# The layer norms' averaging products from f32 to two f16 halves, in a fused FFN and delta-rule attention kernel

## The reference, cut to what matters

```
x = x + 0.5 * ffn(layernorm(x))                 # call "1"
x = x + attn_block(layernorm(x))                # a delta-rule scan over time, 16 heads of 16
x = x + 0.5 * ffn(layernorm(x))                 # call "2"

def layernorm(x):
    m = mean(x, -1);  v = var(x, -1)
    return (x - m) / sqrt(v + 1e-05)

def ffn(x):   # ternary weights, scales s
    h = silu(x @ w1 * s1) * (x @ w2 * s2)
    h = gelu(h @ h1 * s); h = gelu(h @ h2 * s)
    return h @ w3 * s3
```

## Time and profile before

| | |
|---|---|
| median of 3 runs | 1821.66 us (1820.79 to 1822.48) |
| the profiled execution | 1821.63 us, its span 1819.9 us |
| mean granted clock of TensorE | 0.993 of full speed |
| TensorE busy | 1735.8 us, 95% of the span |
| VectorE, GpSimd, ScalarE busy | 68%, 66%, 58% |
| data moved | 23.16 MB, mean 13 GB/s |

### The profile page before, as it was taken

How to read it: one execution, slowest core, us unless ns; L and a number is a source line. 1 busy time by engine, 2 the same in 40 slices (tenths; PEclk the granted TensorE clock), 3 DMA queues, 4 the chain that set the end, 5 groups by cost and what they waited for, 6 DMA issues and landing times.

```text
span 1819.9 us, 29744 instructions
## 1 busy us (share of the span) xinstructions
PE 1735.8 (95%) x10030; PEld 1070.0 (59%) x10030; DVE 1242.6 (68%) x2890; ACT 1059.9 (58%) x2115; POOL 1209.4 (66%) x1501
## 2 busy tenths in 40 slices
PE   6989989999999999999999999999999999999999
PEld 5865555555555555655555555588655555555578
DVE  5255777777776877867777787767776768767331
ACT  4656565465656565646557474757555565655454
POOL 4463876767676666777676667667775867775653
PEclk9999999999999999999999999999999999999999
DMA  7100000000000000000000000000000000000000
GB/s 281 51 1 1 1 1 1 1 1 2 0 2 1 24 1 24 1 1 1 1 1 1 1 24 1 12 13 1 1 1 1 1 1 13 1 1 12 1 13 13
DMA packets 5270, 23.16 MB, mean 13 GB/s; under 512 B 640, under 2 KB 1664, under 8 KB 3584
## 3 DMA queue, kind: packets, MB, share of 16 engines
q1 hardware_dynamic: 5120, 21.26, 3.2%
HBM read 17.06 MB, written 4.19 MB: 12 GB/s over the span
## 4 chain that ended last, share of the span: by engine, by line
PE 64%; issue 10%; POOL 10%; DVE 9%; ACT 7%; DMA 0%; POOLq 0%; DVEq 0%; ACTq 0%; SPq 0%
PE ffn_bank L1072 38%; PE ffn_bank L1055 7%; PE att_bank L1120 5%; PE att_bank L1092 4%; POOL hid_lo L564 4%; POOL pairs_lo L601 2%; PE state_bank L1128 2%; POOL pairs L593 2%; PE ln_bank L1023 2%; PE att_bank L1107 2%; PE att_bank L1108 2%; ACT hid L679 1%; DVE roots L798 1%; DVE hid L820 1%; PE att_bank L1137 1%
## 5 line engine op out<-in xcount | busy, mean ns | idle before, releaser
L1072 PE MATMUL ffn_bank<-hid_hi,w_sb 128*128 128x512 f16 (+1 forms) x2736 | 907.0, 347 | 8.3 <-ACT gate L666 4.7
L1072 PE MATMUL ffn_bank<-hid_lo,w_sb 128*128 128x512 f16 (+1 forms) x2736 | 906.8, 347 | 0.0
L564 POOL TENSOR_TENSOR hid_lo<-hid,hid_hi 128x512 f16<-128x512 f32 (+1 forms) x456 | 462.4, 1029 | 278.3 <-ACT hid_hi L655 277.8
L593 POOL TENSOR_TENSOR pairs<-KQ 128x32 f32<-128x32 f32 (+15 forms) x496 | 326.9, 667 | 146.4 <-DVE KQ L847 104.6
L1072 PEld LDWEIGHTS ffn_bank<-hid_hi,w_sb 128*128 128x128 f16 x2736 | 276.3, 101 | 208.1 <-issue 12.2
L1072 PEld LDWEIGHTS ffn_bank<-hid_lo,w_sb 128*128 128x128 f16 x2736 | 268.9, 98 | 206.3 <-issue 13.6
L601 POOL TENSOR_TENSOR pairs_lo<-pairs,pairs_hi 128x448 f16<-128x448 f32 (+15 forms) x416 | 313.1, 757 | 80.7 <-ACT pairs_hi L727 79.9
L727 ACT CAST pairs_hi<-pairs 128x448 f16<-128x448 f32 (+15 forms) x416 | 176.9, 438 | 200.4 <-POOL pairs L593 147.0
L655 ACT CAST hid_hi<-hid 128x512 f16<-128x512 f32 (+1 forms) x456 | 235.0, 552 | 28.5 <-DVE hid L820 27.8
L679 ACT ACTIVATE hid<-ffn_bank,par_sb 128x512 f32<-128x512 f32 (+1 forms) x304 | 172.2, 616 | 107.6 <-PE ffn_bank L1072 105.2
L1055 PE MATMUL ffn_bank<-xn_hi,w_sb 128*128 128x512 f16 (+1 forms) x608 | 204.8, 351 | 15.1 <-DVE w_sb L769 6.3
(11 more groups left out here) (88 smaller groups left out, 2101.7 us busy)
## 6 DMA issues: line engine op xcount, KB each, us to landing
NK<-in_w SPq DMA_DIRECT2D x11, 1024.0 KB, 6.3
X<-in_x SPq DMA_DIRECT2D x7, 512.0 KB, 3.5
out<-X SPq DMA_DIRECT2D x7, 512.0 KB, 2.6
wqkvb_sb<-in_wqkvb SPq DMA_DIRECT2D x1, 1024.0 KB, 9.1
X<-in_x SPq DMA_DIRECT2D x2, 256.0 KB, 6.7
out<-X SPq DMA_DIRECT2D x2, 256.0 KB, 2.1
wout_sb<-in_wout SPq DMA_DIRECT2D x1, 256.0 KB, 9.9
par_sb<-in_par SPq DMA_DIRECT2D x1, 24.0 KB, 2.5
```

The lines of the kernel that those rows point to most:

```text
L564: pool.tensor_tensor(hid_lo[layer % 2][:, m, call.cols], hid[:, u % 3, call.cols], hid_hi[layer % 2][:, m, call.cols], ALU.subtract).then_ ...
L593: pool.tensor_tensor(packed(pair(pairs, q, dot), n), later, earlier, ALU.mult).then_inc(pairs_made if dot in SPLIT else pairs_ready, 1)
L1072: mm = nc.tensor.matmul(ffn_ps(call, j), weight(name, kk, 2 * pair + i), v[:, kk, cols], start=kk == 0 and part == 0, stop=kk == KT_FF - 1 ...
```

## The change

- The norms in frames (33 of 35) no longer give the f32 sum to TensorE. ScalarE copies feature_sum to an f16 tile `sum_hi`, GpSimd subtracts to get the f16 rest `sum_lo`, and TensorE makes two f16 products with an f16 `average16`, which add up in the bank. So does the variance.
- The additions `sum` and `sq_sum` of the 17 FFN norms in frames go from GpSimd to VectorE. Those of the attention's and the head's norms stay.
- Ticks: the attention norm's `var` stands one tick later; half_ln is laid out anew (16 ticks to `low` where it was 15); the FFN norms of frames 1 and 4 stand at tick 55, not 52; the dot of step 6 of qk at 16, not 17; the copies to Kz two ticks earlier.
- `terms` is one buffer, not two. The qk dots take the matrix of minus ones, as the kk dots do, and O subtracts them. `average` lies in U_sb, which is free at that time. One small reduction at the start is gone (`side_ones`), and the f16 copy made there is that of `average`.

```diff
-E_QK = [1, 4, 6, 7, 12, 14, 17, 19, ...]
+E_QK = [1, 4, 6, 7, 12, 14, 16, 19, ...]
 def ffn_ln(at):
-    return dict(sum=at, mean=at + 4, center=at + 5, square=at + 6, sq_sum=at + 7, var=at + 11, root=at + 11,
+    return dict(sum=at, sum_hi=at + 1, sum_lo=at + 2, mean=at + 4, center=at + 5, square=at + 6, sq_sum=at + 7, sq_hi=at + 8, sq_lo=at + 9, var=at + 11, root=at + 11,
...
-LN_ATT = dict(sum=18, mean=22, center=24, square=25, sq_sum=27, var=30, root=32, recip=35, norm=37, y_recip=38, apply=38, low=39)
+LN_ATT = dict(sum=18, sum_hi=19, sum_lo=20, mean=22, center=24, square=25, sq_sum=27, sq_hi=28, sq_lo=29, var=31, root=32, recip=35, norm=37, y_recip=38, apply=38, low=39)
-LN_FFN = [(-1, 55), (0, 55), (1, 52), (2, 55), (4, 52), (5, 55), ...]
+LN_FFN = [(-1, 55), (0, 55), (1, 55), (2, 55), (4, 55), (5, 55), ...]
...
+        def on_pool(job):
+            return job.kind == "att" or job.frame is None
...
@@ gpsimd
-                if part == "sum":
+                if part == "sum" and on_pool(job):
...
-                if part == "sq_sum":
+                if part == "sq_sum" and on_pool(job):
...
+                if part in ("sum_lo", "sq_lo") and job.frame is not None:
+                    pool.wait_ge(ln_sum_hi, split_count(i, part))
+                    pool.tensor_tensor(sum_lo[:, cols], feature_sum[:, cols], sum_hi[:, cols], ALU.subtract).then_inc(ln_sum_lo, 1)
@@ scalar
+                if part in ("sum_hi", "sq_hi") and job.frame is not None:
+                    if part == "sum_hi":
+                        act.wait_ge(ln_summed, i + 1)
+                    else:
+                        act.wait_ge(ln_sq_summed, i + 1)
+                    act.copy(sum_hi[:, cols], feature_sum[:, cols]).then_inc(ln_sum_hi, 1)
...
-                        if e == E_RETR[c] + 8:
+                        if e == E_RETR[c] + 6:
                             make_kz(f, c)
@@ vector
+                if part == "sq_sum" and not on_pool(job):
+                    dve.wait_ge(ln_squared, i + 1)
+                    nc.vector.tensor_tensor(total, xn[:, 0:1, cols], xn[:, 1:2, cols], ALU.add).then_inc(ln_sq_summed, 1)
...
-                part = terms[:, m % 2, 0:2 * GB * n].rearrange("p (v g w) -> p v g w", v=2, g=GB)
+                part = terms[:, 0:2 * GB * n].rearrange("p (v g w) -> p v g w", v=2, g=GB)
...
-                nc.vector.tensor_tensor(O[:, mine], O[:, mine], O_in[:, :], ALU.add).then_inc(o_ready, 1)
+                nc.vector.tensor_tensor(O[:, mine], O[:, mine], O_in[:, :], ALU.subtract).then_inc(o_ready, 1)
@@ tensor
-                if part in ("mean", "var"):
-                    nc.tensor.matmul(ln_bank[:, 0:cols.stop - cols.start], average[:, :], feature_sum[:, cols], start=True, stop=True).then_inc(ln_filled, 1)
...
+                elif part in ("mean", "var"):
+                    pe.wait_ge(ln_sum_lo, split_count(i, part))
+                    nc.tensor.matmul(ln_bank[:, 0:n], average16[:, :], sum_hi[:, cols], start=True, stop=False)
+                    nc.tensor.matmul(ln_bank[:, 0:n], average16[:, :], sum_lo[:, cols], start=False, stop=True).then_inc(ln_filled, 1)
```

More of the change, by code:

```diff
@@ L306, in build @@
         U_sb = sb("U_sb", [P, COLS])
+        average = U_sb[:, 0:P]
         O = sb("O", [P, COLS])
@@ L319, in build @@
         Uz = sb("Uz", [P, GP, 2, 32])
-        terms = sb("terms", [P, 2, 2 * GB * C])
+        terms = sb("terms", [P, 2 * GB * C])
         state_bd = sb("state_bd", [P, GB, P])
@@ L365, in slab, with split_count @@
             return X[:, s % RING, :, cols]
+        def on_pool(job):
+            return job.kind == "att" or job.frame is None
+        def split_count(i, part):
+            return (i - len(JOB_HEAD)) * 2 + (1 if part in ("sum_hi", "sum_lo", "mean") else 2)
         def both(ap):
@@ L784, in ln @@
                 n = cols.stop - cols.start
+                total, xs = feature_sum[:, cols].unsqueeze(1), slab(job.s, cols)
+                if part == "sum" and not on_pool(job):
+                    if job.kind == "ffn1":
+                        dve.wait_ge(x_loaded, 16 * job.s)
+                    else:
+                        dve.wait_ge(att_read_v, READ["out", job.s * HALVES + (cols.stop - 1) // HALF, 0])
+                    dve.wait_ge(ln_normed, i)
+                    nc.vector.tensor_tensor(total, xs[:, 0:1, :], xs[:, 1:2, :], ALU.add).then_inc(ln_summed, 1)
+                if part == "sq_sum" and not on_pool(job):
+                    dve.wait_ge(ln_squared, i + 1)
+                    nc.vector.tensor_tensor(total, xn[:, 0:1, cols], xn[:, 1:2, cols], ALU.add).then_inc(ln_sq_summed, 1)
                 if part == "center":
@@ L1013, in ln @@
                 i, cols = job.i, job.cols
[L1015 to L1023 removed]
+                n = cols.stop - cols.start
+                if part == "mean" and i:
+                    pe.wait_ge(ln_read, i * 2)
+                if part in ("mean", "var") and job.frame is None:
+                    if part == "mean":
+                        pe.wait_ge(ln_summed, i + 1)
+                    else:
+                        pe.wait_ge(ln_sq_summed, i + 1)
+                    nc.tensor.matmul(ln_bank[:, 0:n], average[:, :], feature_sum[:, cols], start=True, stop=True).then_inc(ln_filled, 1)
+                elif part in ("mean", "var"):
+                    pe.wait_ge(ln_sum_lo, split_count(i, part))
+                    nc.tensor.matmul(ln_bank[:, 0:n], average16[:, :], sum_hi[:, cols], start=True, stop=False)
+                    nc.tensor.matmul(ln_bank[:, 0:n], average16[:, :], sum_lo[:, cols], start=False, stop=True).then_inc(ln_filled, 1)
             def bank_free(call, j):
@@ L1105, in dots @@
                 if dot in SPLIT:
-                    i, ones = SPLIT[dot], head_ones16 if dot[0] == "qk" else head_minus16
-                    nc.tensor.matmul(ps[:, 0:n], ones[:, :], pair(pairs_hi, i, dot), start=True, stop=False)
-                    nc.tensor.matmul(ps[:, 0:n], ones[:, :], pair(pairs_lo, i, dot), start=False, stop=True).then_inc(att_filled, 1)
+                    i = SPLIT[dot]
+                    nc.tensor.matmul(ps[:, 0:n], head_minus16[:, :], pair(pairs_hi, i, dot), start=True, stop=False)
+                    nc.tensor.matmul(ps[:, 0:n], head_minus16[:, :], pair(pairs_lo, i, dot), start=False, stop=True).then_inc(att_filled, 1)
                     return
-                nc.tensor.matmul(ps[:, 0:n], (head_ones if dot[0] == "qk" else head_minus)[:, :], pair(pairs, DOT[dot], dot), start=True, stop=True).then_inc(att_filled, 1)
+                nc.tensor.matmul(ps[:, 0:n], head_minus[:, :], pair(pairs, DOT[dot], dot), start=True, stop=True).then_inc(att_filled, 1)
             def retrieve(w, c):
```

34 lines of the change are left out of this document (13 added, 21 removed).

## The result

| | before | changed |
|---|---|---|
| median | 1821.89 us (1820.79 to 1822.48) | 1847.7 us (1843.85 to 1849.85) |
| ratio | | 1.0138 [1.0126, 1.0151] |
| profiled execution, its span | 1821.63, 1819.9 us | 1847.51, 1845.8 us |
| mean granted clock | 0.993 | 0.990 |

The change costs 26 us. I had said 7 us faster and a range up to 1829: wrong in sign and outside the range. (Times are medians of undisturbed executions; one of e1_f32's five took 5100.91 us and is left out, so its median is 1814.04 us, where the expectations on record have 1815.85.)

A forecast was written before the change was run, and what follows sets the result against it. TensorE, 95% busy and 64% of the chain, was taken as the bound. -19.8 + 5.6 + 2.1 + 2.6 + 2.5 + 1.7 - 1.6 = -6.9 us gave 1814.7 us, range 1801 to 1829.

The forecast's parts named there:

- Loads: Added copies, subtractions and additions on ScalarE, GpSimd and VectorE: costed at nothing outside named places, as idle time covers them.
- The attention's norms: Variance's product a tick later, more than the added links take: 1.6 us of waits for the sum vanish, -1.6.
- What is lost at once: Half of the FFN norms' TensorE saving turns into waiting for pairs_lo: 5.6 us lost, bounds 0 and 11.2.
- Late halves: Places where the low half reaches TensorE's norm product late: frame 8 +2.1, other FFN norms +2.5 us.
- Frame 8: Its norm's copy and subtraction queue behind gelus, hid_hi and hid_lo; TensorE waits 3 to 4 us: term +2.1.
- The terms +2.1, +2.5 and -1.6: Frame 8's late half, some ten other late FFN halves, and the attention's vanished waits for the sum, in us.
- over 20: Sign against the forecast: sum_lo heads TensorE's waits with over 20 us.
- The rival with late halves: Variance's low half late in most FFN norms, 8 of 13, 1.7 us each: 1828.4 us; chance 17%.
- Frame 4: Norm three ticks later, so TensorE waits 2.6 us for xn_lo at call 6: +2.6, bounds 0 and 3.5.
- the rival of the collision: VectorE's moved additions collide with GpSimd, up to 0.96 us longer each: 1821 us, no change; chance 8%.
- The clock: A long TensorE wait in frame 4 or 8 brings one 1.2 GHz stretch: +1.7 us, bounds 0 and 3.4.
- 19.8 us off TensorE: 26 wide and 40 narrow norm products at half their time: 11.2 + 8.6 us less, bounds 0 and 19.8.

The follow-up runs named there:

- e1_f32: Changed kernel with the one f32 product per norm back and no halves; VectorE's additions, new ticks and single buffer stay: 1814.04 us.
- n1_pe: e1_f32 with each of the 66 f32 products made as two f16 products of constant tiles, no wait for a half, averages wrong: 1804.25 us.
- p1_free: h1_copies with the copies' waits for the norms' sums taken out; each waits only for the copy before: 1819.3 us.
- h1_copies: e1_f32 plus 66 unused ScalarE copies of a constant tile, each behind the wait for its norm's sum: 1833.6 us.
- h2_both: h1_copies plus 66 unused GpSimd subtractions, each behind a wait for its copy; TensorE takes the f32 sum: 1847.86 us.
- q2_subfree: e1_f32 plus 66 unused GpSimd subtractions of constant tiles, each waiting only for the one before: 1828.35 us.
- e3_nolow: Changed kernel without GpSimd's subtraction; TensorE takes the high half twice, so the averages are wrong: 1822.32 us.
- m1_att: e1_f32 with halves for the attention's norms alone, 32 of the 66 hand-overs: 1831.22 us.
- k1_oldticks: e1_f32 with the ticks from before the change, except half_ln's, and frame 4's norm at 54: 1818.18 us.
- r3_all_late: h1_copies with the unused copies of both the attention's and the FFN norms two ticks later: 1820.28 us.
- s1_sq16: e1_f32 with ScalarE writing the variance's squares in f16 and TensorE averaging them by two f16 products, without a second sum: 1805.47 us.

## Why the prediction was wrong

The time in pieces, measured one by one but for the last:

| step | us |
|---|---|
| additions on VectorE, new ticks, one buffer (e1_f32) | -7.9 |
| TensorE's shorter products (n1_pe against e1_f32) | -9.8 |
| 66 copies on ScalarE: own time (p1_free against e1_f32) | +5.3 |
| ScalarE held at them (h1_copies against p1_free) | +14.3 |
| 66 subtractions on GpSimd (h2_both against h1_copies; q2_subfree has 14.3 without a hand-over) | +14.3 |
| left for TensorE's waiting for the halves: 1847.7 less (1847.86 - 9.8) | +9.6 |
| sum, against 1822 | +25.8 |

The last line but one is a remainder. It has a check of its own: from e1_f32, less 9.8, plus 19.6 for the copies, e3_nolow should take 1823.8, and it took 1822.3; the changed kernel lies 25.4 above it, which is the subtractions' 14.3 and 11.1 of waiting for the halves. The pieces add within 1.5 us here, but e1_f32's doubt of 3 us is in the first three and in the remainder, and m1_att's 17.2 us come only roughly from shares of them (its waits at the copies 9.4, their own time 2.1, the subtractions 5.4, less 3.4 for TensorE, make 13.5, and 18.6 with the 5.1 us that TensorE waits there for sum_lo).

**Loads: the step that failed.** "None is at its limit ... I cost the load at nothing outside the places above." 34 us in this table stand against that nothing, 19.6 for the instructions themselves and 14.3 for ScalarE's standing at its copies, and they make up the whole distance of 33 us between 1814.7 and 1847.7; the other terms' errors cancel. The lengths of the copies and subtractions were right or even generous (VectorE's 34 additions take 29.7 us in place of "about 20"); the cover was not there. An engine that is 58 or 66% busy over the span isn't free at a given place, since pieces of its row are awaited by other engines. My own bound "without it" (10% of the chain times 45 us, 4.5 us) was no bound: it priced GpSimd at its chain share of before, but q2_subfree shows 14.3 us for 57.8, 25%, and the share itself went from 10 to 16%. And I gave ScalarE no such bound.

**The added waits.** I asked whether TensorE would wait for the halves, and never what is queued behind ScalarE's copy while it waits for the sum. The attention's norms were "no cost", because the low half had two ticks left. It was mostly in time for TensorE; but ScalarE reached its copy up to 4.6 us before GpSimd's sum was there, with pairs_hi and the gelus behind it. By the shares above that is more than half of m1_att's 17 us. The sum's place in GpSimd's row behind the dots was to be read in the orders; I read only the end of the chain.

**What is lost at once: too small.** 5.6 forecast, 10.0 measured (n1_pe), bounds 0 and 11.2. That the saved time turned into waits is argued: TensorE's waits from 130 to 1750 us are 57.6 us in n1_pe and 52.2 in p1_free, which shows some 5 of the 10.

**Late halves.** Frame 8 was right in its mechanism and its size (4.16 against 3.9 us). The terms +2.1, +2.5 and -1.6 made 3.0 us; the remainder is 9.6. Waiting at the norms' products in the steady part is 18.2 us, just short of the "over 20" at which I called the forecast wrong, and three of the attention's variances wait 1.2 us each, where I had "no waits worth the name". The rival with late halves (1828.4) had the right place: 8 of the 13 wide variances wait, as it said, but most for 0.2 to 1.7 us and only frame 8's for 4.2. It had only a part of the price: without the copies' and subtractions' cost it couldn't reach the time.

**Frame 4.** The wait at call 6 is 4.9 us, and I had 2.6 as a term. It comes from the tick and not from the halves: p1_free, where TensorE waits for no half, has the same 4.86 us, and k1_oldticks, a tick earlier, 3.23. But e1_f32 has these ticks and isn't slower than k1_oldticks: the term was mis-sized for the wait, and no cost of it shows in the sum. Frame 4's tick was not run alone.

**VectorE's additions.** 0.95 us in place of 0.69, as the rival of the collision had it possible; they still gain, some 4 us without halves and 19 with them, where I had counted no gain for the move. The Trainium skill ("GPSIMD Engine Reference", Key points) says that VectorE's instructions with two SBUF inputs contend with GpSimd for SBUF. The changed kernel's trace agrees. Of its 26 wide additions, the 5 with no GpSimd instruction beside them all take 0.68 or 0.69 us; the 21 with one take 0.68 to 1.35, and 18 of them 0.85 or more. One of each kind, GpSimd idle at the first and busy at the second:

```profile
1521.78 0.69 DVE L813 TENSOR_TENSOR roots<-xn 128x512 f32<-128x512 f32 x1 [1.12 <-ACT xn L653]
```

```profile
685.17 1.35 DVE L810 TENSOR_TENSOR roots<-X 128x512 f32<-128x512 f32 x1
```

**The clock.** The mean granted clock went from 0.993 to 0.990. Of the spans that is 12.7 us and 18.5 us below full speed: some 6 us more, against 1.7 forecast. But single executions spread, 0.996 in p1_free and 0.991 in r3_all_late, whose times differ by 1 us. How much of each piece above the clock carries stays open; it is not a further piece beside them.

**Right**: 19.8 us off TensorE, by the starts of the products; frame 8's wait. Kz, the buffer and the sign, at zero in the forecast, were not run alone; all ticks together stand at some -4 us.

Not tried: the halves with the attention's dots moved on GpSimd, so that the sum would be early.

## What to carry to other kernels

- An engine that isn't the bound still has a price for each inserted instruction. Here GpSimd, 66% busy, took 14.3 us for 58 us of free-standing work, and ScalarE, 58% busy, 5.3 us for 32. Price inserted work by a share of its length, and don't stop at idle time.
- For each new hand-over ask two questions: when is the result there for who needs it, and how long does the engine that makes it stand before it, with what behind it. The second cost 14 us here, and a look at when TensorE needs the result doesn't find it. Unused copies with and without the wait separate the two.
- Before splitting an f32 operand into halves, look for a producer that can write f16 itself (s1_sq16): it takes instructions away instead of adding two for each.
